# Attention head ends: unscaled accumulator out by VectorE, join and scaling on GpSimd with reciprocal sums spread by two DMAs

## What is computed

```python
q = x @ Wq + bq; k = x @ Wk + bk; v = x @ Wv + bv     # 8 heads of 64 columns
scores = jnp.einsum('bdsh,bdth->bdst', q, k) / SCALE
weights = jax.nn.softmax(scores, axis=-1)
feats = jnp.einsum('bdst,bdth->bdsh', weights, v)
feats = feats.transpose(0, 2, 1, 3).reshape(B, S, F)
return feats @ Wo + bo
```

## Time and profile before

| what | us |
|---|---|
| median of 3 runs (1290.95 to 1292.9) | 1292.33 |
| profiled execution, first to last instruction (span) | 1289.5 |
| attention loop, 132 to 943 us of the span | 811 |
| PE busy in it | 804.9 |
| DVE, ACT, POOL busy in it | 699.2, 661.9, 323.9 |
| experts' stage, 943 to 1206 us | 263 |

### The profile page before, as it was taken

The page is one execution under the profiler, slowest core; times in us unless marked ns, Lnnn a source line. Parts: engine busy times, 40 slices in busy tenths (PEclk is TensorE's granted clock), DMA queues, the critical chain, the costliest instruction groups (busy, mean ns, idle before and its releaser), DMA issues. The chain is left out here.

```text
span 1289.5 us, 24161 instructions
## 1 busy us (share of the span) xinstructions
PE 1255.7 (97%) x8128; PEld 1058.8 (82%) x8128; DVE 998.2 (77%) x1891; ACT 919.8 (71%) x1643; POOL 513.2 (40%) x508
## 2 busy tenths in 40 slices
PE   7999999999999999999999999999988999999896
PEld 5888799889889889989989989989866877777642
DVE  5623688789889979979979979979866777776387
ACT  5421589778878868868868868878833877778343
POOL 0002223234524524524533533542543666676412
PEclk9999999999999999999999999999999999999999
DMA  8788466212424424323423423543578999997698
GB/s 282 258 283 289 155 196 223 69 42 84 147 66 138 145 70 139 125 88 110 146 84 101 155 89 88 156 136 120 178 272 326 386 386 385 346 339 252 237 426 335
DMA packets 90951, 253.14 MB, mean 196 GB/s; under 512 B 16824, under 2 KB 39480, under 8 KB 87504
## 3 DMA queue, kind: packets, MB, share of 16 engines
q1 hardware_dynamic: 70608, 196.78, 44.9%
q0 software_dynamic: 17920, 50.62, 10.2%
q10 hardware_dynamic: 2304, 4.20, 0.8%
HBM read 177.87 MB, written 134.91 MB: 243 GB/s over the span
## 5 line engine op out<-in xcount | busy, mean ns | idle before, releaser
L967 ACT ACTIVATE p_hi<-slot 128x512 fp32r<-128x512 f32 x512 | 278.5, 596 | 108.9 <-PE slot L1594 105.5
L807 POOL TENSOR_TENSOR p_lo<-prob,p_hi 128x512 fp32r<-128x512 f32 x128 | 166.1, 1297 | 441.9 <-ACT prob L969 441.7
L1607 PE MATMUL slot<-k_stack,q_stack 128*128 128x512 f32 x1024 | 300.1, 415 | 0.0
L984 ACT ACTIVATE prob<-prob,row_min 128x1024 f32<-128x1024 f32 x256 | 296.8, 1160 | 0.1
L1307 DVE TENSOR_TENSOR p_lo<-slot,p_hi 128x512 fp32r<-128x512 f32 x384 | 250.8, 681 | 52.5 <-ACT p_hi L967 51.1
L1594 PE MATMUL slot<-ident,prob 128*128 128x128 f32 x2048 | 265.8, 273 | 1.3 <-ACT prob L984 1.3
L1632 PE MATMUL pv_acc<-p_hi,v_pair 128*128 128x256 f32 x1024 | 263.1, 290 | 2.6 <-POOL p_lo L807 1.8
L1632 PE MATMUL pv_acc<-p_lo,v_pair 128*128 128x256 f32 x1024 | 253.7, 281 | 0.0
L1594 PEld LDWEIGHTS slot<-ident,prob 128*128 128x128 f32 x2048 | 229.5, 141 | 1.9 <-issue 1.7
L1632 PEld LDWEIGHTS pv_acc<-p_hi,v_pair 128*128 128x128 f32 x1024 | 192.6, 188 | 16.1 <-issue 5.7
L1632 PEld LDWEIGHTS pv_acc<-p_lo,v_pair 128*128 128x128 f32 x1024 | 192.8, 188 | 12.9 <-issue 3.3
(11 more groups left out here) (196 smaller groups left out, 1974.4 us busy)
## 6 DMA issues: line engine op xcount, KB each, us to landing
disp_hbm<-zero_hbm SPq DMA_DIRECT2D x64, 518.0 KB, 6.3
rows_all<-disp_hbm SPq DMA_DIRECT2D x64, 518.0 KB, 12.8
y_hbm<-zero_hbm SPq DMA_DIRECT2D x48, 512.0 KB, 4.4
got<-y_hbm SPq DMA_DIRECT2D x15, 1536.0 KB, 19.0
q_stack<-q_hbm SPq DMA_DIRECT2D x128, 128.0 KB, 3.1
up_pair<-in_L_ffn_w_up SPq DMA_DIRECT2D x26, 512.0 KB, 9.5
down_w<-in_L_ffn_w_down SPq DMA_DIRECT2D x32, 256.0 KB, 12.0
q_hbm<-q_hi SPq DMA_DIRECT2D x8, 512.0 KB, 2.7
```

The source lines that it names most:

```text
L807: e.tensor_tensor(p_lo[1][:, 2:4, :], prob[:, m % 2, :, (4 * u + 2) * P:(4 * u + 4) * P], p_hi[1][:, 2:4, :].bitcast(F32), ALU.subtract).t ...
L967: e.activation(p_hi[b][:, two, :], view[:, two, :], ACT.Copy).then_inc(a_phi, 1)
L984: e.activation(keys, keys, ACT.Exp, bias=row_min[:, me % 2, j, 1:2], scale=-1.0, accum_out=row_sum[:, me % 2, j, half:half + 1]).then_inc( ...
L1607: made = e.matmul(slot[:, n * BANK:(n + 1) * BANK], qs[:, part, j * P:(j + 1) * P], k_stack[:, ms % H, keys], start=part == 0, stop=part == 1)
```

## The change

PE's two transposes per head and ACT's copy go away. DVE copies `pv_acc` to `acc` as it is. SP stores `row_inv` (128 x 2) to HBM and reads it back spread over 64 partitions (`inv_all`), two DMAs per head. The move of the upper half is issued one step later, the join runs one step later, and behind it POOL multiplies by `inv_all`, read with a step of two elements. `moved`, `feats` and `resid` are doubled, so some waits refer to an older chunk. The chunk-end jobs begin three ticks later on all engines. The zeroing DMAs of SP, one a step before, are grouped in the first two steps of a head, the others stand in step 1. The scratch for GpSimd's DMA descriptors is cut to 4096.

```diff
+        inv_hbm = hbm("inv_hbm", (2, P, QT))
...
-        P0, P1 = 14, 38
+        P0, P1 = 17, 41
...
+            def store_inverse(m):
+                e.wait_ge(v_inv, m + 1)
+                if m >= 2:
+                    e.wait_ge(d_spread, 16 * (m - 1))
+                e.dma_start(inv_hbm[m % 2], row_inv[:, :]).then_inc(d_inv, 16)
+
+            def spread_inverse(m):
+                e.wait_ge(d_inv, 16 * (m + 1))
+                if m >= 2:
+                    e.wait_ge(g_scaled, m - 1)
+                e.dma_start(inv_all[m % 2][0:D, :],
+                            inv_hbm[m % 2].rearrange("p j -> (p j)").partition_broadcast(D)).then_inc(d_spread, 16)
...
-                mj, uj = divmod(s - LAG - 2, STEPS)
+                mj, uj = divmod(s - LAG - 3, STEPS)
                 if mj >= 0 and uj == STEPS - 1:
-                    e.wait_ge(v_scaled, mj + 1)
+                    joined = moved[mj % 2][0:D, :]
+                    e.wait_ge(v_acc_out, mj + 1)
                     e.wait_ge(d_moved, 16 * (mj + 1))
-                    e.wait_ge(p_proj, 2 * (mj // H))
-                    target = moved[0:D, :] if mj % 2 else feats[0:D, (mj % H) // 2, :]
-                    e.tensor_tensor(target, scaled[0:D, :], moved[0:D, :], ALU.add).then_inc(g_join, 1)
+                    e.tensor_tensor(joined, acc[0:D, :], joined, ALU.add).then_inc(g_join, 1)
+                    c, k = mj // H, (mj % H) // 2
+                    if c >= 2:
+                        e.wait_ge(p_proj, 2 * (c - 1))
+                    e.wait_ge(g_join, mj + 1)
+                    e.wait_ge(d_spread, 16 * (mj + 1))
+                    e.tensor_tensor(
+                        (joined if mj % 2 else feats_of(c)[0:D, k, :]).rearrange("d (j p) -> d j p", j=QT),
+                        joined.rearrange("d (j p) -> d j p", j=QT),
+                        inv_all[mj % 2][0:D, :].rearrange("d (p j) -> d j p", j=QT), ALU.mult).then_inc(g_scaled, 1)
...
-                if 0 <= r < LAST and u == 3:
-                    e.wait_ge(p_spread, m + 1)
-                    if m:
-                        head_out(e, m - 1)
-                    e.activation(scaled[:, :], misc[:, 0:QC], ACT.Copy).then_inc(a_spread, 1)
...
-                    e.wait_ge(a_spread, mv + 1)
-                    e.wait_ge(p_pv, 4 * mv + 4)
+                    e.wait_ge(p_pv, STEPS * (mv + 1))
                     if mv:
-                        head_out(e, mv - 1)
-                    e.tensor_tensor(scaled[:, :], pv_acc[:, 0:QC], scaled[:, :], ALU.mult).then_inc(v_scaled, 1)
+                        e.wait_ge(g_join, mv)
+                    e.tensor_copy(acc[:, :], pv_acc[:, 0:QC]).then_inc(v_acc_out, 1)
...
                     e.wait_ge(a_exp, 4 * m + 4)
+                    if m:
+                        e.wait_ge(d_inv, 16 * m)
...
-                if 0 <= r < LAST and u == 3:
-                    e.wait_ge(v_inv, m + 1)
-                    wait_misc()
-                    for j in range(QT):
-                        made = e.transpose(misc[:, j * P:(j + 1) * P], row_inv[:, j:j + 1].to_broadcast([P, P]),
-                                           ident[:, :])
-                    made.then_inc(p_spread, 1)
-                    misc_read.append((a_spread, m + 1))
...
-    nc = _bacc.Bacc("TRN2", target_bir_lowering=False, num_devices=1)
+    nc = _bacc.Bacc("TRN2", target_bir_lowering=False, num_devices=1, dynamic_dma_scratch_size=4096)
```

More of the change, by code:

```diff
@@ L165, in build @@
         scat = [sb(f"scat{j}", [P, TOPK], U32, att) for j in range(2)]
+        moved.append(sb("moved1", [P, QC], F32, att))
+        feats.append(sb("feats1", [P, H // 2, QC], F32, att))
+        inv_all = [sb(f"inv_all{i}", [P, QC], F32, att) for i in range(2)]
+        resid += [sb(f"resid{i}", [P, WITH], F32, att) for i in range(QT, 2 * QT)]
         att.close()
@@ L216, in build @@
         p_k, p_q, p_v = (sem(f"pe_{n}") for n in ("k", "q", "v"))
-        p_scores, p_turned, p_pv, p_spread = (sem(f"pe_{n}") for n in ("scores", "turned", "pv", "spread"))
+        p_scores, p_turned, p_pv = (sem(f"pe_{n}") for n in ("scores", "turned", "pv"))
         p_proj, p_x1t, p_gate, p_rank = (sem(f"pe_{n}") for n in ("proj", "x1_turned", "gate", "rank"))
@@ L220, in build @@
         a_xhi, a_whi, a_khi, a_qhi, a_vhi = (sem(f"act_{n}") for n in ("x_hi", "w_hi", "k_hi", "q_hi", "v_hi"))
-        a_exp, a_phi, a_copy, a_spread = (sem(f"act_{n}") for n in ("exp", "p_hi", "p_copy", "spread"))
+        a_exp, a_phi, a_copy = (sem(f"act_{n}") for n in ("exp", "p_hi", "p_copy"))
         a_x1t, a_score = sem("act_x1_turned"), sem("act_score")
@@ L225, in build @@
             "x_lo", "w_lo", "k_lo", "q_lo", "v_add", "v_lo"))
-        v_min, v_lo, v_sum, v_inv, v_scaled = (sem(f"dve_{n}") for n in ("min", "p_lo", "sum", "inverse", "scaled"))
+        v_min, v_lo, v_sum, v_inv, v_acc_out = (sem(f"dve_{n}") for n in ("min", "p_lo", "sum", "inverse", "acc_out"))
         v_resid, v_norm = sem("dve_resid"), sem("dve_norm")
@@ L403, in head_out, with feats_of @@
             else:
-                e.wait_ge(g_join, m + 1)
+                e.wait_ge(g_scaled, m + 1)
+        def feats_of(c):
+            return feats[c % 2]
         def keys_under_rows(n):
@@ L760, in chunk_end @@
                 to = ticks()
-                yield from to(10)
+                yield from to(13)
                 root(c, 0)
@@ L801, in gpsimd @@
             jobs = []
-            for s in range(LAST + LAG + 2):
+            for s in range(LAST + LAG + 4):
                 r = s - LAG
@@ L1569, in chunk_end @@
                 to = ticks()
-                yield from to(5)
+                yield from to(8)
                 out_project(c, 0)
-                yield from to(9)
+                yield from to(12)
                 out_project(c, 1)
```

70 lines of the change are left out of this document (41 added, 29 removed).

## The result

| | us |
|---|---|
| kernel before, median of 5 runs | 1292.33 |
| changed kernel, median of 5 runs (1313.07 to 1322.38) | 1316.15 |
| ratio, with its 95% interval | 1.0193 (1.0168 to 1.0219) |
| profiled execution after: span, granted clock | 1320.6, 0.988 |

What follows compares the result with a forecast made beforehand. PE was taken to bound the attention loop. Against the span of 1289.5 us, -13.5 + 4.4 + 4.4 = -4.7 gave 1284.8, and with 2.8 between span and median 1287.6; range 1280 to 1294.

Steps and rivals of the forecast that it cites:

- The transposes, -13.5: Head ends on PE: removing two transposes saves 0.21 to 0.22 us a head, 13.5 us in all.
- SP, "some 10, hidden": SP's store and spread per head: 4 to 13 us from 4.5 on, taken as done at some 10, before POOL multiplies.
- End of the loop, "0.5 are left. No loss": Last `feats` DMA, behind the multiply: with 2.0 us to land, spare time falls from 1.3 to 0.5, nothing lost.
- main case: Whole kernel: the forecast sum, 1287.6 us, own range 1284 to 1291; chance 0.42.
- Rival (c): POOL's multiply takes 1.29 us: 16.4 us more in four places, 1304.0; chance 0.17 with weaker forms.
- POOL, tile 1's scatters, +4.4: Behind tile 1's four scatters and the bias, POOL's `p_lo` starts 0.85 us late in six chunks: 4.4 us lost.
- POOL, tile 0's scatters, "nothing lost": Behind tile 0's scatters, POOL's `p_lo` comes in time by 0.17 us, so nothing is lost.
- DVE, marking behind the multiply, +4.4: Routing in the loop: DVE's marking waits for POOL's multiply, PE waits 0.3 to 0.4 us for 14 tiles: 4.4 us.
- The multiply at 0.73: POOL's multiply, read with a step of two elements, costs what the join does, 0.73 us.
- scratch at 0: Cutting the descriptor scratch to 4096 bytes costs 0, with up to 1 us kept in the range.
- A wait in heads without any routing: Sign in the loop that the prediction is wrong: PE waits in heads that have no routing; no size given.
- Rival (d): Spread sums land late and hold POOL's queue: 1 us late costs up to 64, giving 1351.6; chance 0.03.

Runs made afterwards that it cites:

- store_only: The changed kernel without the spread DMA and the division; the store of the sums to HBM and the wait for it stay: 1313.9 us, ratio 1.0169.
- pair_in_sbuf: The changed kernel with the reciprocal sums stored to a spare row of `inv_all` in SBUF and spread from there, result complete: 1297.9 us, ratio 1.0045.
- no_pair: The changed kernel without its two new DMAs per head and their waits; POOL multiplies by ones, the division is left out: 1291.3 us, ratio 0.9995.
- bias_early: The changed kernel with the sums stored and spread in SBUF, and POOL adding tile 0's bias four steps earlier: 1291.9 us, ratio 0.9999.
- projection_early: The kernel before with PE asking for tile 0's projection two steps earlier in seven chunks, before `feats` can be there: 1369.4 us, ratio 1.0457.

## Why the prediction was wrong

**The transposes, -13.5.** Right: steps of 2.75 everywhere.

**SP, "some 10, hidden".** This is the step that failed. Hidden was right as to the pair's own wait: store and spread take 3.7 and 4.3 us in the median, 8.0 instead of the 3.8 that I took but within "4 to 13", and the spread has landed 2.3 us or more before the multiply in all 64 heads. What was wrong is that I set the price of the store at nothing beyond that. I asked only when store and spread would land and who waits for them, and took the row of the 64 KB move as the nearest in kind. I did not ask what they do to others, and the attention loop before has no packet of 8 bytes from which to read it. store_only and pair_in_sbuf, against no_pair and the changed kernel, put the store's price at 18 to 23 us.

**End of the loop, "0.5 are left. No loss".** The same 2.0 us to land was used here, and only for the last chunk. For the seven projections in the loop I had no term in the main case, though before too the projection stood near its deadline: it began 1.0 us after the landing in the first chunk, 0.3 in two and 0.1 in four. With 4.7 for 2.0 the waits are 16.1 us in sum; the fall of the clock at the two longest, which I had nowhere, is 4.7 more (6.27 and 5.78 us for eight matmuls that take 3.67 in the other five places). Rival (c) named this place ("`feats` lands some 0.5 after PE wants it in 7") but from a slow multiply, which did not come.

**POOL, tile 1's scatters, +4.4.** Right: the step is 0.88 too long in six chunks, 0.12 before, so 6 x 0.76 = 4.6; bias_early takes it away.

**POOL, tile 0's scatters, "nothing lost".** Wrong by 5.2. POOL itself was in time; what stood still was DVE. I had checked one DVE operation against the multiply, the marking, and left out the score addition that the three ticks moved to the end of an odd step. I had also cited the Trainium skill for two-input instructions only. The same section of the Trainium skill (SBUF — State Buffer, § Who interferes with whom) lists `tensor_scalar` among those that, where their operands allow it, can enter a mode of two ports and so contend with GpSimd; the 1.81 us of L1206, which has one input, agree.

**DVE, marking behind the multiply, +4.4.** The working itself gives 9.45 - 9.04 = 0.41 a tile, so 5.7 and not 14 x 0.31. The size is nearly what the routing steps lost (4.5), the mechanism mostly not: the marking takes 0.55 to 0.58 in 11 of 16 and 1.15 at most, and most of the 4.5 stands behind the blocked addition. A hit by chance.

**The multiply at 0.73**, scratch at 0: right (0.74, ratio 1.0000).

**A wait in heads without any routing** was named as a sign of being wrong, and it came: 3.0 us in two early heads, where `moved` lands late.

**The sum.** Without the pair the loop comes out near the forecast: in no_pair, which keeps all else, it is 4.0 us shorter than before, where 4.7 was forecast. Part of that is luck: tile 0's steps cost 5.2 that I had at nothing, the routing steps some 2 instead of 4.4, and 2.1 came back that I had not counted (the small waits before the projections 1.3, the last head 0.8). The median, 1291.3, is 3.7 above the forecast; the profiled execution (1288.0) is the fastest of ten, and for what the others take more no trace was kept. Rival (d), sums that land late, was the nearest to the truth in kind (a DMA cost) but priced a wait that never occurs; no rival had the DMAs of others. The range should have held a term of 16 to 25 us for seven projections, most of which had a slack of a tenth of a microsecond.

## What to carry to other kernels

A new DMA has two prices, its own landing and what it does to all others in flight; the second is not in the trace of a kernel without it, so list every wait on a DMA whose slack is small against the differences between landing times. Write pieces of a few bytes to SBUF, not to HBM, or try packets of 64 bytes. When jobs are moved by an odd number of half steps, look at each small DVE operation and what POOL runs beside it, and give POOL pairs of scatters rather than fours. Here the store to SBUF, the earlier bias and the pairs together turned +1.9% into -0.7%.

## What the runs showed of the hardware

- 128 packets of 8 bytes to HBM, once in 11 us, bring a 64 KB move within SBUF from 1.9 to 4.9 us and a 128 KB load from 3.0 to 4.3 (no_pair against store_only); beside 128 packets of 64 or of 512 bytes the load takes 3.0 and 3.1. The Trainium skill (DMA: Bandwidth & Descriptors, "Why small descriptors are slow (HBM only)") says that transfers within SBUF don't suffer from small pieces. pair_in_sbuf agrees in the main: its store lands in 1.9 us instead of 3.7, and most of the harm to others is gone. The full rate from 512 bytes on, which the Trainium skill states (the same page, § Specifications), is not where the harm to others ends here.
- POOL instructions that follow each other without a gap keep a waiting DVE instruction out: 1.81 us (multiply and `p_lo`), 2.03 us (bias and `p_lo`), 0.53 behind a single running `p_lo`. This holds for a DVE operation with a single SBUF input too.
- A row of 1 KB spread from one partition of SBUF to 64 lands in 4.1 us, hardly sooner than from HBM (4.3 beside the stores).
- The granted clock fell to 1.2 GHz at all seven idle stretches of PE of 4.4 to 5.1 us, which cost 1.7 us once and 2.7 to 3.0 us six times on the eight 128x512 matmuls behind them (projection_early).
